# Two-layer attention and convolution kernel: broadcasts as 32-row tiles, a new order of a step on all engines, later handling of weights

## What is computed

```python
xn = x / norm * g * C ** 0.5            # x: group-normed image
q, k, v = split(einsum('bchw,oc->bohw', xn, w_qkv))
q = softmax(q, axis=-2) * scale         # over the 32 channels of a head
k = softmax(concat(mk, k), axis=-1)     # over 4 + 4096 positions
context = einsum('bhdn,bhen->bhde', k, concat(mv, v))
x = x + einsum('bchw,oc->bohw', einsum('bhde,bhdn->bhen', context, q), w_out) + b_out
z = gn(x)
x = x + conv3x3(z, w3 * m3) + einsum('oi,bihw->bohw', w1 * ~m3, z) + b.sum(axis=1)
```

## Time and profile of the kernel before

| | |
|---|---|
| median of 3 runs | 2093.57 us (2093.47 to 2094.22) |
| profiled execution, its own time | 2094.91 us |
| its span, first to last instruction | 2093.1 us |
| mean granted clock of TensorE | 0.986 |
| TensorE, VectorE busy | 1958.1 us (94%), 1736.9 us (83%) |
| ScalarE, GpSimd busy | 1353.9 us (65%), 1363.3 us (65%) |

### The profile page before, as it was taken

The page is one execution under the profiler, slowest core; times in us unless marked ns, Lnnn a source line. Parts: engine busy times, 40 slices in busy tenths (PEclk is TensorE's granted clock), DMA queues, the critical chain, the costliest instruction groups (busy, mean ns, idle before and its releaser), DMA issues.

```text
span 2093.1 us, 50607 instructions
## 1 busy us (share of the span) xinstructions
PE 1958.1 (94%) x21199; PEld 1044.2 (50%) x21199; DVE 1736.9 (83%) x3144; ACT 1353.9 (65%) x1476; POOL 1363.3 (65%) x737
## 2 busy tenths in 40 slices
PE   2889999999999999999999999999999999999996
PEld 0445545555544555544555544555544555554552
DVE  5688888888988888988888988888988888888863
ACT  2567666767666666666666666676766676766661
POOL 5566667766667676666676667676666676666662
PEclk9799999999999999999999999999999999999997
DMA  4367767887667878667787667778777778766675
GB/s 104 61 130 150 154 145 154 168 166 152 146 151 155 170 157 165 147 142 154 167 156 164 151 149 147 163 160 172 147 146 151 156 166 167 152 147 148 134 142 125
DMA packets 349427, 312.96 MB, mean 150 GB/s; under 512 B 299152, under 2 KB 299920, under 8 KB 341008
## 3 DMA queue, kind: packets, MB, share of 16 engines
q1 hardware_dynamic: 347712, 308.73, 70.9%
q10 hardware_dynamic: 1168, 0.98, 0.2%
q0 software_dynamic: 320, 0.01, 0.0%
HBM read 68.10 MB, written 67.11 MB: 65 GB/s over the span
## 4 chain that ended last, share of the span: by engine, by line
PE 67%; DVE 21%; ACT 4%; POOL 3%; DMA 2%; issue 1%; SPq 1%; ACTq 0%
PE pair_ps L799 15%; PE pair_ps L781 8%; PE pair_ps L762 7%; DVE km L1111 7%; PE pair_ps L705 5%; PE bank_ps L699 5%; PE pair_ps L790 4%; PE pair_ps L742 4%; POOL exp_kT_lo L447 3%; PE bank_ps L772 3%; PE pair_ps L765 3%; DVE nrm L1098 2%; DVE parts L1098 2%; PE bank_ps L751 2%; DVE u L1108 2%; PE bank_ps L754 2%
## 5 line engine op out<-in xcount | busy, mean ns | idle before, releaser
L799 PE MATMUL pair_ps<-replicas,w_rep 96*32 96x512 f16 x8192 | 488.9, 383 | 8.9 <-DMA replicas<-yg_lo 8.9
L444 POOL TENSOR_TENSOR u_lo<-u,u_hi 128x1024 f16<-128x1024 f32 x128 | 270.0, 2146 | 273.9 <-ACT u_hi L551 273.9
L447 POOL TENSOR_TENSOR exp_kT_lo<-exp_kT,exp_kT_hi 128x1024 f16<-128x1024 f32 x128 | 301.0, 2361 | 179.1 <-ACT exp_kT_hi L560 179.0
L450 POOL TENSOR_TENSOR u_lo<-exp_q,u_hi 128x1024 f16<-128x1024 f32 x128 | 272.5, 2140 | 113.2 <-ACT u_hi L566 113.2
L799 PEld LDWEIGHTS pair_ps<-replicas,w_rep 96*32 96x32 f16 x8192 | 206.1, 96 | 275.4 <-issue 89.4
L1163 DVE SCALAR_TENSOR_TENSOR image<-pair_ps,image 128x512 f32<-128x512 f32 x256 | 172.2, 681 | 121.9 <-PE pair_ps L799 118.2
L440 POOL TENSOR_SCALAR u<-image,st 128x1024 f32<-128x1024 f32 x128 | 187.9, 1479 | 110.4 <-DVE st L1062 110.4
L551 ACT ACTIVATE u_hi<-u 128x1024 f16<-128x1024 f32 x128 | 130.8, 1045 | 177.6 <-DVE u L1108 177.5
L566 ACT ACTIVATE u_hi<-exp_q 128x1024 f16<-128x1024 f32 x128 | 135.3, 1057 | 161.1 <-DVE exp_q L1150 161.0
L557 ACT ACTIVATE exp_kT<-pair_ps,zcol 128x1024 f32<-128x1024 f32 x128 | 141.0, 1101 | 144.4 <-PE pair_ps L742 144.3
L536 ACT ACTIVATE exp_kT<-u,zcol 128x1024 f32<-128x1024 f32 x128 | 146.0, 1143 | 93.7 <-POOL u L440 92.4
(11 more groups left out here) (179 smaller groups left out, 4832.1 us busy)
## 6 DMA issues: line engine op xcount, KB each, us to landing
image<-in_x SPq DMA_DIRECT2D x256, 256.0 KB, 4.8
out<-image SPq DMA_DIRECT2D x512, 128.0 KB, 2.2
replicas<-yg_hi SPq DMA_DIRECT2D x256, 165.0 KB, 3.9
replicas<-yg_hi SPq DMA_DIRECT2D x256, 107.2 KB, 5.1
replicas<-yg_lo SPq DMA_DIRECT2D x128, 165.0 KB, 4.3
replicas<-yg_lo SPq DMA_DIRECT2D x128, 107.2 KB, 3.8
uT_hi<-u_hi SPq DMA_TRANSPOSE x128, 3.4
uT_lo<-u_lo SPq DMA_TRANSPOSE x128, 3.4
```

The lines of the kernel that those rows point to most:

```text
L444: pool.tensor_tensor(px(UL, v), px(U, v), px(UH, v), ALU.subtract).then_inc(ul_ready, 1)
L447: pool.tensor_tensor(KL[:, v % 2], KT[:, v % 2], KH[:, v % 2], ALU.subtract).then_inc(kl_ready, 1)
L450: pool.tensor_tensor(px(EL, v), px(EQ, v), px(EH, v), ALU.subtract).then_inc(el_ready, 1)
L799: mm = pe.matmul(conv_ps[32 * r:32 * r + 32, j % 2], w_rep[0:32 * SLOTS, tap, r], rep[:, j * ROWS + dy:(j + 1) * ROWS + dy, dx:dx + SIDE], ...
```

## The change

The broadcast takes four chunks at a time. A chunk's parts stand on 32 rows, and its matmul uses these rows of `spread` and `parts` alone, each on a row tile of its own, into four PSUM banks of two pairs. There are two broadcasts an image and kind instead of four.

```diff
-            def broadcast(ps, v, done):
-                for j in (2 * v, 2 * v + 1):
-                    mm = pe.matmul(ps[:, (j % 2) * BANK:(j % 2 + 1) * BANK], spread[:, j], parts[:],
-                                   start=True, stop=True)
+            def broadcast(v, first_ps, second_ps, done):
+
+                for j in range(4 * v, 4 * v + 4):
+                    ps = (first_ps, second_ps)[j % 4 // 2]
+                    q = slice(32 * (j % 4), 32 * (j % 4) + 32)
+                    mm = pe.matmul(ps[:, (j % 2) * BANK:(j % 2 + 1) * BANK], spread[q, j], parts[q],
+                                   start=True, stop=True, tile_position=(32 * (j % 4), 0))
                 mm.then_inc(done, 1)
```

The order of a step is new on all engines. The new image p now goes on to all rough keys, rough queries 0 and 1 and the turned shift within its step, and the convolution of c is complete in its step. TensorE's step after the change, removed lines left out (semaphore waits too, where they follow from the order):

```diff
+                if a is not None:
+                    rough_q(a, 2, pair_ps[0])
+                    pe.wait_ge(k_max, at(a, 8, 8))
+                    keys(a, 0, pair_ps[2])
...
+                    keys(a, 1, pair_ps[1])
+                    rough_q(a, 3, pair_ps[2])
+                    keys(a, 2, pair_ps[0])
+                    keys(a, 3, pair_ps[1])
+                    turn_q_max(bank_ps[1])
+                    context(a, 0, bank_ps[0])
+                    queries(a, 0, pair_ps[2])
+                    queries(a, 1, pair_ps[0])
+                    context(a, 1, bank_ps[0])
+                    queries(a, 2, pair_ps[1])
+                    conv_dense(c, 0)
+                    group_means(0, bank_ps[1], x_group)
+                    queries(a, 3, pair_ps[0])
...
+                    context(a, 2, bank_ps[0])
+                    conv_ring(c, 0)
+                    conv_dense(c, 1)
+                    context(a, 3, bank_ps[0])
+                    conv_ring(c, 1)
+                    norm_sums(p, 0, bank_ps[1])
+                    turn_context(bank_ps[0])
+                    norm_sums(p, 1, bank_ps[1])
+                    den_broadcast(a, 0, pair_ps[0], pair_ps[1])
+                    value_context(bank_ps[0])
+                    conv_dense(c, 2)
+                    norm_sums(p, 2, bank_ps[1])
+                    mix_weights(bank_ps[0])
+                    den_broadcast(a, 1, pair_ps[0], pair_ps[1])
+                    conv_ring(c, 2)
+                    norm_sums(p, 3, bank_ps[1])
+                    conv_dense(c, 3)
+                    mix(a, 0, pair_ps[0])
+                    mix(a, 1, pair_ps[1])
+                    conv_ring(c, 3)
+                    mix(a, 2, pair_ps[0])
+                    conv_dense(c, 4)
+                    conv_ring(c, 4)
+                    conv_dense(c, 5)
+                    pe.wait_ge(norm_dve, at(p, 5, 5))
+                    inv_norm(p, 0, pair_ps[0], pair_ps[1])
+                    conv_ring(c, 5)
+                    conv_dense(c, 6)
+                    inv_norm(p, 1, pair_ps[0], pair_ps[1])
+                    conv_ring(c, 6)
+                    mix(a, 3, pair_ps[0])
+                    rough_k(p, 0, pair_ps[1])
+                    conv_dense(c, 7)
+                    pe.wait_ge(y_ready, at(a, UNITS, 4))
+                    rough_k(p, 1, pair_ps[0])
+                    pe.wait_ge(k_max, at(p, 8, 1))
+                    rough_k(p, 2, pair_ps[1])
+                    conv_ring(c, 7)
+                    pe.wait_ge(k_max, at(p, 8, 3))
+                    rough_k(p, 3, pair_ps[1])
+                    pe.wait_ge(out_ready, at(c, CHUNKS, 8))
+                    rough_q(p, 0, pair_ps[2])
+                    pe.wait_ge(k_max, at(p, 8, 4))
+                    rough_q(p, 1, pair_ps[1])
+                    pe.wait_ge(k_max, at(p, 8, 7))
+                    turn_k_max(bank_ps[1])
```

```diff
+                    normalise(p, 0, pair_ps[0])
+                    normalise(p, 1, pair_ps[1])
+                    finish(c, 5)
+                    normalise(p, 2, pair_ps[0])
+                    normalise(p, 3, pair_ps[1])
+                    finish(c, 6)
+                    residual(a, 3, pair_ps[0])
+                    max_k(p, 0, pair_ps[1])
+                    max_k(p, 1, pair_ps[0])
+                    max_k(p, 2, pair_ps[1])
+                    finish(c, 7)
+                    max_k(p, 3, pair_ps[1])
+                    shift_k(p)
+                    max_q(p, 0, pair_ps[2])
+                    row_k(p, bank_ps[1])
```

Setup:

```diff
+            load(0, 0)
+            load(0, 1)
+            for h in range(2):
+                sp.wait_ge(x_in[h][0], at_load(0))
+            load(1, 0)
+            load(1, 1)
...
+            act.wait_ge(weights_in, 16 * WEIGHT_DMAS)
+            act.activation(perm_qkv, raw_qkv.rearrange("p t (i r) -> p t r i", r=RES), ACT.Copy).then_inc(setup_act, 1)
+            act.activation(perm_w1, raw_w1.rearrange("p (i r) -> p r i", r=RES), ACT.Copy).then_inc(setup_act, 1)
+            for t in range(TAPS):
+                last = act.activation(perm_w3[:, t], raw_w3.rearrange("p (i r t) -> p t r i", r=RES, t=TAPS)[:, t], ACT.Copy)
...
             def norm_guard(s, ps):
 
                 dve.tensor_scalar(nrm[:], ps[:], 1e-24, None, ALU.max).then_inc(norm_dve, 1)
+                if first(s):
+                    split_conv_weights()
```

499 lines of the change are left out of this document (214 added, 285 removed).

## The result

| | before, same chip | after |
|---|---|---|
| median of 4 runs | 2093.89 us (2093.47 to 2094.27) | 2112.45 us (2111.80 to 2112.57) |
| profiled execution, its own time | 2094.91 us | 2112.38 us |
| its span | 2093.1 us | 2110.6 us |

The account below looks back on a forecast made before the run. TensorE was taken as nearest to the bound, VectorE close behind and its series setting the second half. Intervals +27, first interval -2, start -8, end -2: +15 us, on the median of 2093.57 giving 2109 us; range 2057 to 2145.

Parts of the forecast that it names:

- First half: From the start of keys to the end of the first mix, TensorE nearly without a gap: 41.8 falls to 39.5 us.
- the wait on the denominators' split stays as it is: First half: TensorE's wait for that split unchanged, its chain being the same but for one high part of y in front.
- Second half: From the end of the first mix to the next image's keys: VectorE's series 21.9 us plus waits, together 23.8.
- GpSimd's last low part of the queries now falls on the second split, +0.4 (bounds 0 and 0.8): Second half: GpSimd's low part overlaps VectorE's second norm split and adds 0.4 us an image.
- comes 1.1 us later behind a maximum that nobody needs so soon: Second half: row of the shift 1.1 us later on VectorE, behind the first maximum over queries; given as the loss.
- Norm sums: First half, TensorE: four separate quarters instead of two of them together, +0.98 us an image.
- Start: Before the intervals: weights at 18, first broadcast at 38 instead of 47.4, 1 given back: -8 us (bounds -3 and -14).
- End: Last image: its y seed no longer waits for the previous image's rings 6 and 7, -2 us (bounds -4, +3).
- TensorE the bound: Whole interval: TensorE stays the bound throughout, interval 61.6 us, time 2057 us; chance 0.20.
- Tiles nearly free: Broadcasts: 0.22 us a group, all four groups on the path, interval 62.2, time 2076 us; chance 0.13.
- Gains and losses cancel: Whole interval: 62.8 us, time 2090 to 2098 us; chance 0.09.
- No overlap: Broadcasts: row tiles do not run side by side, 1.07 us a group, interval 65.6, time 2178 us; chance 0.08.

Follow-up runs that it names:

- run 3: Changed kernel with ScalarE's high part 3 of the queries moved right behind high part 2, ahead of the norms' logarithm: 2077.91 us.
- run 4: Changed kernel with high part 3 of the queries early, plus one useless GpSimd instruction per image meant to run beside the second norm split: 2115.17 us.
- run 7: Changed kernel with high part 3 early, row of the shift before the first maximum over queries (pairs swapped), GpSimd's low y 3 before x's group norm: 2078.99 us.
- run 2: Kernel before, order and setup untouched, with each pair of broadcasts on two row tiles side by side: 2046.58 us.
- Run 9: Changed kernel with high part 3 of the queries early, norm sums 2 beside 3 and 0 beside 1, minus_max behind the first low parts: 2059.15 us.
- run 5: Changed kernel with norm sums 2 moved behind ring 2, directly ahead of norm sums 3, as before the change: 2098.15 us.
- run 8: Changed kernel with GpSimd's minus_max made behind the first image's low parts of u instead of behind its first step: 2109.47 us.
- run 1: Changed kernel in its new order, but each broadcast matmul again over all 128 rows instead of row tiles: 2170.17 us.
- run 6: Changed kernel with the row of the shift ahead of the first maximum over queries on VectorE, pairs swapped to match: 2139.86 us.

## Why the prediction was right, and where it was off

**The result** (2109 forecast, 2112.45 measured) is as close as it is by luck. The two halves of the interval were off by 0.95 us too much and 0.9 too little, each worth some 28 us over the run. Start and first interval gained 5 us less than forecast. On the profiled execution the +15 us of the forecast were +27 for the intervals, -10 for start and first interval, -2 for the end; the +17.5 measured are +23.8, -5.1 and -1.2.

**Interval.** Forecast +0.9; from the third turned maximum on (179.5 and 184.6 us) the intervals are 63.23 and 62.41 us, +0.82. By halves:

- *First half*, forecast 39.5, measured 38.55. Three terms were too high. A group costs 0.33, not 0.5 (0.35 for two). The stall of 0.3 before the group means of x did not come. And "the wait on the denominators' split stays as it is" was wrong: its 0.5 us is covered by the norm sums and the shorter path ahead of it. (The split itself did stay as it was, 5.08 us before and 5.10 after.) Together 1.1.
- *Second half*, forecast 23.8, measured 24.7. The failed step is "GpSimd's last low part of the queries now falls on the second split, +0.4 (bounds 0 and 0.8)". The place was right and the size was not: the cast was held 1.45 us, and taking the collision away gives 1.15 (run 3), putting one back costs it again (run 4). I took the price from the slow instruction at 1024.38, 0.8 us over the quick one. But a held instruction doesn't run at a slower rate: it waits until GpSimd's ends, so the bound was what is left of GpSimd's 2.1 us. Without the collision the series is 23.5; my sum for that is 23.4.

**The reason given for the loss.** I wrote that the row of the shift "comes 1.1 us later behind a maximum that nobody needs so soon". That was wrong. Keys 0 writes pair 2, which only that maximum sets free; and with the order turned around and the pairs swapped the time stays (run 7, where GpSimd's low y 3 was moved too). What does hold is that VectorE's series sets the second half: it is busy 23.1 of 24.7 us, TensorE 21.3. But that series alone would have left the change faster than before: the collision costs 34.5 us (2112.45 against 2077.91), and the tiles, the rest of the order and the setup together gain 16. The order has a price beyond the collision: from the third turned maximum on run 3's interval is 62.03 us and run 2's, in the old order, 60.84. Run 9 gives 0.52 of these 1.19 us to the norm sums; the other 0.67 are open.

**Norm sums** +0.98 an image on TensorE: as forecast in size, but only some 0.3 us of it on the path; the rest covered waits (runs 5 and 9).

**Start.** Forecast -8; the first turned maximum came 0.7 us earlier and the first interval was 4.3 shorter (forecast -2; its reason, that this one has no convolution, was not tested). The weights landed at 18.94 (forecast 18). "GpSimd's minus_max moves behind its first step: nothing" failed: 3.5 us on the path by the same collision (run 8). And the new order costs the first image time that I hadn't counted: from first broadcast to first turned maximum it is 14.2 us after and 11.1 before. Each group of four is followed by a wait of TensorE for two `normalise` (2.46 us), but that makes only 0.3 of the 3.1. The rest comes behind the last `normalise`: before, VectorE went on to the maxima of the keys without a gap, and after it waits twice for rough keys, 1.13 us each, and the turned maximum starts 0.45 us after the shift instead of at once. **End:** forecast -2, measured -1.2 (from L824's last start to the end of the span 97.4 us, before 98.6).

**Rivals.** (1) *TensorE the bound*: its interval of 61.6 comes close to run 3's 61.93, so without the collision this rival's number would have been near, and the forecast's 62.9 too high by its error in the first half. Run 3 shows both bounds in turn: TensorE has no gap in the first half and waits 2.3 us for VectorE in the second. (2) *Tiles nearly free*: half right on the price (0.33 against 0.22 and 0.5), not on the sum. The Trainium skill's 3.07 times (TensorE: Matmul & The Clock Gate, Measured speedup vs the span model) agrees with 0.97 over 0.32, 3.0 times, each with its change of mode in it. (3) *Gains and losses cancel*: excluded, the interval is over 62.8 us. (4) *No overlap*: excluded; that kernel takes 2170 us, forecast 2178.

**Signs.** The turned maxima are 63.23 us apart (forecast 63.3), a group takes 0.32 instead of 0.5, and the second split is followed by the longest gap. TensorE does not wait before the turned maximum (forecast 0.5), but before the rough keys and queries (0.29, 0.53, 0.26 and 0.51 us), and 0.68 us before the keys (forecast 1.0).

## What to carry to other kernels

Here the row tiles paid at once when put in alone (47 us): try that before reordering anything. When an order changes, lay GpSimd's timeline beside VectorE's and look for VectorE's casts from SBUF to SBUF, and its instructions with two inputs in SBUF, that start under a GpSimd instruction: price each at what is left of the GpSimd instruction, not at a rate, and check it after every shift, since it comes and goes with fractions of a microsecond. It can also hide in a comparison that is meant to measure something else, as in runs 1 and 5. Where one engine's series and another's work take turns as the bound, a piece of work moved across the border only changes halves.

## What the runs showed of the hardware

- A cast from SBUF to SBUF on VectorE that starts while a GpSimd instruction runs ends behind it: a cast of 0.42 us took 1.87, 1.86 and 2.38 and ended 0.28 us after GpSimd's, one of 0.29 took 2.48 beside a memset and ended 0.15 after it. So does an instruction with two inputs in SBUF: a subtraction of 0.43 took 4.85 (0.26 after), the second instruction of a split 2.43 and 1.57 instead of 0.75 (0.54 after).
- A cast that started 0.09 us ahead of GpSimd's low part, with 0.13 us of the group norm left, took its 0.43 us (1027.73). Within 0.1 us of the change from one GpSimd instruction to the next it went both ways: 0.41 us at 1026.97 in the kernel before, 2.38 at 1039.21 in run 6.
- Instructions with one input in SBUF and another in PSUM, and the statistics, which read one SBUF tensor, are not held. In the changed kernel 65 `residual`, 66 `normalise` and 243 statistics start at least 0.15 us ahead of the end of a running GpSimd instruction, and none takes longer than 1.29, 1.22 and 0.69 us, as when GpSimd is idle.
- Two and four row tiles of 512 columns cost the same from start to start, 0.32 us, and four full matmuls in the same place 0.97.
- Two kernels that differ in one pair of norm sums had mean granted clocks of 0.985 and 0.975; the lower mean comes from eight falls to the lower level, 34 us in all, between 216 and 1886 us, where the other kernel's clock never fell.
